# The fold of the output projection, sixteen heads in a row, split into four groups of four heads over the quarters of a tile

## The reference

```python
sq = elu_plus_one(q)                            # elu(q) + 1
sk = elu_plus_one(k)
kv = jnp.einsum('bhsd,bhse->bhde', sk, v)       # one 128x128 matrix a head
qkv = jnp.einsum('bhsd,bhde->bhse', sq, kv)
norm = jnp.einsum('bhsd,bhd->bhs', sq, sk.sum(axis=2))
attn = qkv / (norm[..., None] + EPS)
return attn.transpose(0, 2, 1, 3).reshape(b, s, H * D) @ Wo.T
x = x + _layernorm(_L0_attn_ref(_layernorm(x), ...))
```

## Time and profile before

| | us |
|---|---|
| median of 3 runs | 2469.23 (2468.17 to 2470.07) |
| the profiled execution | 2465.01 |
| its span | 2463.3 |
| PE busy | 2234.5 (91%) |
| DVE, ACT, POOL busy | 1487.0, 1237.6, 956.6 |
| mean granted TensorE clock | 0.962 of full |

### The profile page before, as it was taken

How to read it: one execution, slowest core, us unless ns; L and a number is a source line. 1 busy time by engine, 2 the same in 40 slices (tenths; PEclk the granted TensorE clock), 3 DMA queues, 4 the chain that set the end, 5 groups by cost and what they waited for, 6 DMA issues and landing times.

```text
span 2463.3 us, 64597 instructions
## 1 busy us (share of the span) xinstructions
PE 2234.5 (91%) x11850; PEld 1922.4 (78%) x11851; DVE 1487.0 (60%) x4836; ACT 1237.6 (50%) x2643; POOL 956.6 (39%) x1128
## 2 busy tenths in 40 slices
PE   7999799999989999995698999989999898989980
PEld 5887488888858888884588988878889787978970
DVE  4555467777767777775555555565554555555546
ACT  3344456666655666663344454555444544454433
POOL 1212015555525555556333333333334333333432
PEclk9999899999999999997799999999999999999995
DMA  3234102333333333333897888888777777777767
GB/s 121 85 120 126 61 26 100 120 118 116 126 127 115 129 108 118 119 130 129 251 225 186 184 205 177 189 197 177 149 154 140 187 154 154 140 170 147 139 110 294
DMA packets 165230, 358.64 MB, mean 146 GB/s; under 512 B 21168, under 2 KB 21168, under 8 KB 165040
## 3 DMA queue, kind: packets, MB, share of 16 engines
q0 software_dynamic: 60512, 144.74, 28.4%
q1 hardware_dynamic: 91216, 173.89, 23.3%
q10 hardware_dynamic: 13440, 39.33, 4.8%
HBM read 178.21 MB, written 179.66 MB: 145 GB/s over the span
## 4 chain that ended last, share of the span: by engine, by line
PE 38%; issue 4%; DMA 3%; ACTq 3%; ACT 2%; DVE 1%; POOL 1%; DVEq 1%; SPq 0%; POOLq 0%
PE bank L465 7%; PE bank L467 6%; PE bank L466 6%; PE bank L456 4%; PE bank L482 3%; PE bank L486 2%; PE bank L475 2%; PE bank L484 2%; PE bank L483 2%; PE bank L485 2%; DMA LATE<-w_in 1%; DMA RAW<-w_in 1%; ACTq L325 1%; POOL sorted_rows L1525 1%; ACT WB L333 1%
## 5 line engine op out<-in xcount | busy, mean ns | idle before, releaser
L1459 POOL DMA_INDIRECT moe_sum<-Y,aidx x276 | 432.1, 1565 | 783.6 <-DMA moe_sum<-Y,aidx 404.0
L929 PE MATMUL bank<-WB,XH 128*128 128x512 f32 x1536 | 477.3, 392 | 0.0
L465 PE MATMUL bank<-WB,XL 128*128 x1104 | 399.5, 362 | 0.0
L467 PE MATMUL bank<-WB,XH 128*128 x1104 | 373.9, 339 | 0.0
L466 PE MATMUL bank<-WB,XH 128*128 x1104 | 372.3, 337 | 0.0
L929 PEld LDWEIGHTS bank<-WB,XH 128*128 128x128 f32 x1536 | 290.7, 189 | 58.3 <-issue 0.5
L929 PE MATMUL bank<-WB,XL 128*128 128x512 f32 x768 | 316.0, 411 | 10.4 <-DVE XL L1241 10.4
L929 PE MATMUL bank<-WB,SH 128*128 128x512 f32 x1024 | 317.3, 391 | 0.0
L709 DVE SCALAR_TENSOR_TENSOR BIG<-BIG,bank x276 | 95.9, 347 | 357.1 <-ACT BIG L527 270.5
L1525 POOL DMA_INDIRECT sorted_rows<-BIG,pos x256 | 265.7, 1038 | 94.6 <-issue 94.6
L527 ACT ACTIVATE BIG<-bank x276 | 91.4, 331 | 346.2 <-PE bank L467 320.3
(11 more groups left out here) (215 smaller groups left out, 4266.8 us busy)
## 6 DMA issues: line engine op xcount, KB each, us to landing
BIG<-sorted_rows SPq DMA_DIRECT2D x278, 274.0 KB
Y<-x_in SPq DMA_DIRECT2D x64, 256.0 KB, 2.8
RAW<-w_in ACTq DMA_DIRECT2D x15, 768.0 KB
LATE<-w_in ACTq DMA_DIRECT2D x15, 768.0 KB
sorted_rows<-BIG SPq DMA_DIRECT2D x33, 274.0 KB
moe_sum<-LATE SPq DMA_DIRECT2D x34, 256.0 KB, 3.0
LATE<-x_in SPq DMA_DIRECT2D x32, 256.0 KB
RAW<-wo_in SPq DMA_DIRECT2D x16, 512.0 KB, 3.5
```

What stands on the lines that cost most here:

```text
L465: nc.tensor.matmul(eu[s][:, 0:UP], XL[:, s, k, :], wh, start=k == 0, stop=False)
L467: last = nc.tensor.matmul(eu[s][:, 0:UP], XH[:, s, k, :], wl, start=False, stop=k == KC - 1)
L929: last = nc.tensor.matmul(ps, w, m, start=start and i == 0, stop=stop and i == len(terms) - 1)
L1459: nc.gpsimd.indirect_dma_start(acc_dram[:, :], bass.IndirectOffsetOnAxis(aidx[:, s:s + 1], 0), rows, None, compute_op=ALU.add).then_inc(s_ ...
```

## The change

The fold's turn (four transposes and the copy) moves ahead of Q in quarter 0. The sixteen heads go in four groups, group g in quarter g of the tile, each between T and O. In tile 0 the heads alternate over the two `po` banks, which are free there; in tile 16, where `po` holds the tile before, over the `pq` banks, beginning with the one that the chunk before has left. In tile 16 the turned kv matrices have a place of their own (`kvt[1]`); before, both folds used that of `x2t`. In tile 16, Q waits for the low parts of the group before.

```diff
-        kvt = kvs0[:, 0:HID].rearrange("p (h n) -> p h n", h=KV_HEADS)
-        x2t = kvt
+        kvt = [t[:, 0:HID].rearrange("p (h n) -> p h n", h=KV_HEADS) for t in (kvs0, kvs1)]
+        x2t = kvt[0]
...
+        def fold_bank(b, h):
+
+            return po[h % 2][:, :] if b == 0 else pq[(h // GROUP + 1 + h) % 2][:, :]
...
-                pe.wait_ge(s_xl, TILES + BATCH_TILES * b + 2)
+            def fold_turn(b):
+
+                pe.wait_ge(s_xl, TILES + BATCH_TILES * b + 1)
                 for h in range(KV_HEADS):
                     last = nc.tensor.transpose(pt[:, h * P:(h + 1) * P], kvs[b][:, h, 0:HEAD_DIM], ident[:, :])
                 last.then_inc(s_kt, 1)
+
+            def fold_group(b, g):
+
                 pe.wait_ge(s_ktc, b + 1)
-                pe.wait_ge(s_zq, 64 * b + 4)
-                for h in range(HEADS):
+                for i in range(GROUP):
+                    h = g * GROUP + i
+                    if b and i < 2:
+                        pe.wait_ge(s_zq, 4 * BATCH_TILES * b + g + i)
                     if h >= 2:
                         pe.wait_ge(s_mlo, HEADS * b + h - 1)
...
-                pe.wait_ge(s_mlo, HEADS * (b + 1))
...
+                        if fixed and c == 0 and t in (0, BATCH_TILES):
+                            fold_turn(b)
...
+                        if fixed and b and 0 < j - 4 * BATCH_TILES <= CHUNKS:
+                            pe.wait_ge(s_mlo, HEADS + GROUP * (j - 4 * BATCH_TILES))
...
-                    if fixed and c == 3 and t in (0, BATCH_TILES):
-                        fold(b)
+                    if fixed and t in (0, BATCH_TILES):
+                        fold_group(b, c)
+                        if c == 3:
+                            pe.wait_ge(s_mlo, HEADS * (b + 1) if b == 0 else HEADS + GROUP)
```

More of the change, by code:

```diff
@@ L998, in _ @@
             pe.wait_ge(s_wg, 32)
-            def fold(b):
-                pe.wait_ge(s_xl, TILES + BATCH_TILES * b + 2)
+            def fold_turn(b):
+                pe.wait_ge(s_xl, TILES + BATCH_TILES * b + 1)
                 for h in range(KV_HEADS):
@@ L1013, in fold @@
                         pe.wait_ge(s_raw[h // 2 % 2], base + 16 * (h // 4 + 1))
-                    nc.tensor.matmul(pq[h % 2][:, :], kvt[:, h // GROUP, :], raw2[h // 2 % 2][:, (h % 2) * HID:(h % 2 + 1) * HID],
+                    nc.tensor.matmul(fold_bank(b, h), kvt[b][:, h // GROUP, :], raw2[h // 2 % 2][:, (h % 2) * HID:(h % 2 + 1) * HID],
                                      start=True, stop=True).then_inc(s_m, 1)
-                pe.wait_ge(s_mlo, HEADS * (b + 1))
             def b_body(t, s, b):
@@ L1140, in _, with fold_turn, fold_group @@
             kv_out(1)
-            def fold(b):
+            def fold_turn(b):
                 act.wait_ge(s_kt, b + 1)
-                nc.scalar.activation(kvt[:, :, :].rearrange("p h n -> p (h n)"), pt[:, :], ACT.Copy).then_inc(s_ktc, 1)
-                for h in range(HEADS):
+                nc.scalar.activation(kvt[b].rearrange("p h n -> p (h n)"), pt[:, :], ACT.Copy).then_inc(s_ktc, 1)
+            def fold_group(b, g):
+                for h in range(g * GROUP, (g + 1) * GROUP):
                     act.wait_ge(s_m, HEADS * b + h + 1)
-                    nc.scalar.activation(m_hi[:, h * HID:(h + 1) * HID], pq[h % 2][:, :], ACT.Copy).then_inc(s_mhi, 1)
+                    nc.scalar.activation(m_hi[:, h * HID:(h + 1) * HID], fold_bank(b, h), ACT.Copy).then_inc(s_mhi, 1)
             def b_body(t, s, b):
@@ L1297, in _, with fold_group @@
             dve.wait_ge(s_wg, 32)
-            def fold(b):
-                for h in range(HEADS):
+            def fold_group(b, g):
+                for h in range(g * GROUP, (g + 1) * GROUP):
                     dve.wait_ge(s_mhi, HEADS * b + h + 1)
                     cols = slice(h * HID, (h + 1) * HID)
-                    nc.vector.tensor_tensor(m_lo[:, cols], pq[h % 2][:, :], m_hi[:, cols].bitcast(f32), ALU.subtract).then_inc(s_mlo, 1)
+                    nc.vector.tensor_tensor(m_lo[:, cols], fold_bank(b, h), m_hi[:, cols].bitcast(f32), ALU.subtract).then_inc(s_mlo, 1)
             def norm_rec(j, i, b, c):
```

## The result

| | before | after |
|---|---|---|
| median, 6 runs each | 2466.43 us (2462.19 to 2470.07) | 2453.06 us (2444.29 to 2459.33) |
| ratio of the two | | 0.9950, 95% interval 0.9931 to 0.9969 |
| the profiled execution, its span | 2465.01, 2463.3 | 2444.98, 2443.3 |

The account below looks back on a forecast made before the run. Stage B was taken as bound by PE, with idle time to win around the folds. Gains of 8.4 us (tile 16) and 3.6 (tile 0) sum to 12.0, giving 2457.2 us from the median; range 2451 to 2464.

Parts of the forecast that it names:

- Bound and place: Stage B is bound by PE; what can be won is PE's idle time around the folds in tiles 0 and 16.
- Tile 16, 8.4 forecast: Tile 16: 26.4 us removed, 18.0 added (turn 0.6, four groups of 4.26, 0.4 for the norm), a gain of 8.4.
- Tile 0, 3.6 forecast: Tile 0: gain 6.3 us with the clock held, less 2.7 for clock falls; bounds 6.3 and, with three falls, 0.6.
- The schedule with the clock held: Tile 0: O starts 34.4 us after PE is free of the first Q, against 41.3 before.
- a gap of 3.7: Tile 0, group 1: PE idles 3.7 us before the second pair, its high parts queued on ACT behind scaling and norm.
- The falls of the clock: Tile 0: each fall behind a gap costs 1.7 to 1.9 us; one and a half falls taken, 2.7 us.
- the turn was to cost 0.6: Tile 0: the turn adds 0.6 us ahead of the first Q, and the clock's rise behind it does not move.
- In-order queues: ACT and DVE take instructions strictly first in, first out, so tile 0's parts wait behind the chunk's own work.
- The 28.3 us: Tile 0: if ACT could take high parts when due, the three gaps would be 0.8 each and O start at 28.3.
- The second rival: Tile 0: the clock falls at every gap and gives its gain back; total gain 9.0 us, 2460.2; chance 0.15.
- The third and fourth: Third: waits only move to Q and T, 2467, chance 0.05. Fourth: parts delay SH and next groups, slower, 2479, chance 0.03.
- The third rival's price: Idle time turns up at Q and T, each group losing 2.5 us more: 2467; chance 0.05.

Follow-up runs that it names:

- only0b: The changed kernel with four groups in tile 0 only, tile 16 keeping sixteen heads in a row; ratio 0.9986 to the kernel before, tile 0 46.42 us.
- again: The changed kernel run once more with no edit, beside the kernel before; ratio 0.9957, tile 0 47.73 us, tile 16 43.84 us.
- groups_two_pairs: The changed kernel loading only the first two pairs of Wo per fold, reused for the other six; tile 0 48.28 us, tile 16 43.84 us.
- warm: The changed kernel with 12, 4 and 8 unread matmuls filling PE's gaps in groups 1 to 3 of tile 0; ratio 0.9928, tile 0 44.26 us.
- defer: The changed kernel with scaling and next input's norm behind the group's high parts on ACT in tile 0; ratio 0.9963, tile 0 45.88 us.
- order2: The changed kernel with tile 0's high parts ahead of SH on ACT, low parts ahead of SL on DVE; ratio 0.9944, tile 0 43.41 us.
- halves: Tile 0 queues as in order2, plus T between each group's two pairs in both fold tiles; ratio 0.9928, tile 0 39.47 us, tile 16 42.58 us.

## Why the prediction was right, step by step

The place, the waits and the queues were right. That the sum, 12.0, came so near the timed 12.3 is in part luck: what the two tiles measured differs between executions by 1.6 us in tile 16 and by 2 in tile 0, and the errors in tile 0 have opposite signs.

- Bound and place: right. The loops between the folds take the same time to 0.1 us in all kernels, and all that the change does is in tiles 0 and 16.
- Tile 16, 8.4 forecast, 8.6 measured. The way of a group was right (2.54 forecast from pair to pair, 2.51 measured; the norm of the input costs 0.26 in quarter 1, 0.4 forecast). The turn and the groups took 43.87 - (52.48 - 26.43) = 17.8, 18.0 forecast. No load is waited for, and no Q waits for a low part. But what was taken away was misread in part: 1.0 of it was the slow clock in the row of before. The prediction named that fall and gave it no term; against only0b's row, with the clock held and its loads 0.6 less late, the gain is 50.86 - 43.86 = 7.0.
- Tile 0, 3.6 forecast, 5.2 measured (5.8 in again, 7.1 in only0b, 5.3 in groups_two_pairs), inside the bounds of 0.6 to 6.3 but for one. Three terms were mis-sized, not all in one direction. The schedule with the clock held was to take 34.4 us from the first head to the first O; warm, where it is held, took 32.9. I had laid the rows end to end, while on ACT and DVE an instruction that waits for nothing else starts about 0.1 us before the row ahead ends (264.43 + 0.80 against 265.14); I estimate some fifteen such places along that chain, and a gap of 3.7 was 2.8. The falls of the clock were to cost 2.7; there were two, and they cost 3.5 to 4.1. Third, the turn was to cost 0.6 ahead of the first head, with the clock's rise where it was. The rise moved: 5.84 us from the norm matmul to the first head with the turn in it, 6.65 to the end of the same Q before without it, so 0.8 gained in place of 0.6 lost. That is luck and not the change: in only0b, defer and order2 the same way took 6.9 to 7.1. In the profiled execution the three terms make +1.5, -1.3 and +1.4, together the 1.6 us between 3.6 and 5.2.
- In-order queues: shown. What stands ahead of the parts on ACT sets the gap in group 1 and what stands ahead on DVE that in group 2; with both moved the gaps are 0.6 to 0.8. The Trainium skill's sentence on the two queues ("TensorE: Matmul & The Clock Gate", Architectural detail) agrees with these rows. The 28.3 us that I gave for queues without order is not what rearranging both queues gives, 30.7 (order2, 255.33 to 286.01); with T between the pairs as well it is 28.25 (halves, 254.61 to 282.86).
- The second rival, that the clock falls at every gap and takes tile 0's gain back, did not come: the clock fell behind two gaps of three and 5.2 us were left, and with one fall (only0b) 7.1. Warm sizes it. The third and fourth, that the waits come back at Q and T or that tile 16 gets worse, did not come either: in tile 16 the only new wait is 1.1 us of the weight loads for the bias add, in four places. The third rival's price was added up wrongly: 2.5 us more for each group, of which there are eight, is 20 and gives 2477, not 2467; the forecast and the range don't use it.

## What to carry to other kernels

A ladder of small dependent steps through three engines (matmul, high part, low part) costs its round for every pair when it stands alone, and only once a group when it is cut and laid between work that does not need it; its loads are then hidden. Cutting it puts it into in-order queues ahead of other chains, so look on each engine at what stands before the first piece of every group, and put there what nobody waits for yet. Where gaps of some us stay on PE, price the clock with them: here the cheap cure, 24 matmuls into a free bank, gave 3.5 to 4.1 us of tile 0, over a quarter of the change's own 13.8.

## What the runs showed of the hardware

- The same gap does not always bring the clock down. Ahead of the second pair of group 3 of tile 0 it fell behind 1.97 us (after) and 1.99 (again) and held through 1.96 in the same group of only0b. Else it fell behind gaps of 2.06 (defer, group 2), 2.24 (before, tile 16), 2.84 and 3.50, and behind the two of 1.75 and 1.57 ahead of stage B, and held through 2.31 (defer, group 3, PEclk 1.00 from 284 to 290) and 1.69 (only0b). How long it then stays at 1.2 GHz differs between executions (5.62 and 5.84 us for the same turn and Q in two of the same kernel; 7.1 with the same instructions in order2).
- The experts, unchanged, scatter by 15 us between executions, stage B by 0.1 us outside the stretches in which the clock falls. A small change in attention is read better from its stretch than from the whole.
